# Local-attention layers on one core: the scores in tiles of 64 rows by 32 columns from one dense copy of the keys

## The reference, cut to what matters

```python
q, k, v = split(x @ Wqkv)                    # each [8, 16 heads, 512, 64]
q = rotary(l2norm(q) * qs); k = rotary(l2norm(k) * ksc)
# windows of 32 queries; each looks at its own 32 keys and the 32 before
bk2 = look(bk)                               # [.., 16 windows, 64 keys, 64]
sim = einsum('bhwie,bhwje->bhwij', bq, bk2) * 8.0
sim = where(mask, -max, sim)                 # only the last 33 keys up to the query
out = einsum('bhwij,bhwje->bhwie', softmax(sim), bv2)
x = out @ Wo + x
```

## Time and profile before

| | before |
|---|---|
| median of three runs | 4502.78 us |
| the profiled execution | 4502.94 us |
| its span (first to last instruction) | 4501.1 us |
| PE matmul busy | 4176.2 us (93%) |
| DVE busy | 4087.6 us (91%) |
| ACT busy | 2794.1 us (62%) |
| POOL busy | 2806.5 us (62%) |
| scores, L1233 | 12288 matmuls, 383.6 us |

### The profile page before, as it was taken

One profiled execution on the slowest core, in us unless ns is written; L12 is line 12 of the kernel. 1 busy time (PEld: TensorE's weight loads), 2 busy tenths in 40 slices (PEclk: granted clock), 3 DMA queues, 4 the chain that ended last, 5 costly groups with the idle time before them and its releaser, 6 DMA issues. The chain is left out here.

```text
span 4501.1 us, 98228 instructions
## 1 busy us (share of the span) xinstructions
PE 4176.2 (93%) x35048; PEld 2719.8 (60%) x35048; DVE 4087.6 (91%) x5503; ACT 2794.1 (62%) x4035; POOL 2806.5 (62%) x4595
## 2 busy tenths in 40 slices
PE   5999999999879999999999999999999999999997
PEld 3555555555456666666666666666666666666664
DVE  5888888888779999999999999999999999999995
ACT  4666666666545666666666666666666666666663
POOL 3555555555456666667666766666666666666663
PEclk9999999999989999999999999999999999999998
DMA  1000000000010000100011000100001000001000
GB/s 54 3 6 5 3 3 5 5 3 3 17 36 17 16 16 20 36 19 16 15 31 28 15 17 15 32 27 17 17 19 38 17 16 17 19 18 36 16 16 14
DMA packets 173500, 81.29 MB, mean 18 GB/s; under 512 B 109120, under 2 KB 168512, under 8 KB 172224
## 3 DMA queue, kind: packets, MB, share of 16 engines
q1 hardware_dynamic: 173248, 78.08, 6.4%
HBM read 48.56 MB, written 16.91 MB: 15 GB/s over the span
## 5 line engine op out<-in xcount | busy, mean ns | idle before, releaser
L581 POOL TENSOR_TENSOR pn<-es,rden 128x1024 f32<-128x1024 f32 x192 | 366.3, 1908 | 694.0 <-DVE rden L912 694.0
L675 ACT ACTIVATE y<-ps 128x1024 f32<-128x1024 f32 x384 | 372.2, 1021 | 507.4 <-PE ps L1119 507.4
L565 POOL TENSOR_TENSOR t<-t,ardn 128x1024 f32<-128x1024 f32 x256 | 484.6, 1893 | 301.4 <-DVE ardn L797 301.4
L666 ACT ACTIVATE t<-ps,anm,srn 128x512 f32<-128x512 f32 x512 | 392.5, 770 | 274.8 <-DVE anm L806 274.8
L585 POOL TENSOR_TENSOR t<-t 128x1024 f32<-128x1024 f32 x192 | 454.4, 2367 | 88.3 <-DVE t L864 88.3
L864 DVE TENSOR_TENSOR t<-ps,tabl 128x512 f32<-128x512 f32 x768 | 490.5, 680 | 0.0
L862 DVE TENSOR_TENSOR t<-ps,tabl 128x1024 f32<-128x1024 f32 x384 | 466.8, 1216 | 16.6 <-ACT sq L691 13.4
L587 POOL TENSOR_TENSOR t<-t 128x1024 f32<-128x1024 f32 x192 | 452.7, 2358 | 2.4 <-DVE t L864 2.4
L966 DVE TENSOR_TENSOR qn<-t,rn 128x2048 f32<-128x2048 f32 x192 | 438.1, 2282 | 5.1 <-POOL rn L394 5.1
L922 DVE TENSOR_REDUCE ss<-sq 128x32 f32<-128x2048 f32 x192 | 436.6, 2274 | 0.0
L996 PEld LDWEIGHTS ps<-cst,qn 128*128 128x128 f32 x3072 | 350.0, 141 | 114.2 <-issue 58.4
(11 more groups left out here) (138 smaller groups left out, 8859.4 us busy)
## 6 DMA issues: line engine op xcount, KB each, us to landing
tokens_dram<-x SPq DMA_DIRECT2D x96, 128.0 KB
xs<-tokens_dram SPq DMA_DIRECT2D x192, 64.0 KB, 1.8
xw<-tokens_dram SPq DMA_DIRECT2D x192, 64.0 KB, 1.9
xsh<-x SPq DMA_DIRECT2D x48, 128.0 KB
xsh<-x SPq DMA_DIRECT2D x48, 127.0 KB
wm<-in_l_wqk SPq DMA_DIRECT2D x3, 1024.0 KB, 4.9
wv<-in_l_wv SPq DMA_DIRECT2D x6, 512.0 KB, 3.8
wo<-in_l_wo SPq DMA_DIRECT2D x6, 512.0 KB, 4.6
```

Source lines behind the costliest of these rows:

```text
L565: nc.gpsimd.tensor_tensor(eA[:, v], eA[:, v], ardn[:, v].unsqueeze(2).to_broadcast([P, 2, SEQ]), ALU.mult).then_inc(a_pn, 1)
L666: e = act.activation(eA[:, j, h], bank(j % 2 * 2 + h), ACT.Exp, bias=anm[:, j, h:h + 1], scale=srn[:, a % 2, j, h:h + 1], accum_out=aden[: ...
```

## The change

The scores are computed with 64 rows, one head at a time. `kpad` becomes `kT`: 8 pairs x 544 columns, two heads one above the other in the rows as in `qT`, no zeros between. The buffer behind it (`kbuf`) keeps the size that the attention part needs. The two ACT copies of 64 partitions x 1024 become one of 128 x 1024, and the memset covers only the 32 columns before the first window of each pair. Each score matmul takes the 64 rows of one head, 32 queries as weights, and streams 64 key columns; there are 64 of them in a turn (128 instructions) in place of 32 (64 instructions). Even heads go to the first bank of pool1, odd heads to the second, so that scores and everything behind them stand in the order of `slot`, and the fold's result is read straight.

```diff
-        kpad = sb("kpad", [P, H, WIN + SEQ])
+        kbuf = sb("kbuf", [P, 4 * NU * SEQ])
+        kT = kbuf[:, 0:PAIRS * (WIN + SEQ)].rearrange("p (a c) -> p a c", a=PAIRS)
-            nc.gpsimd.memset(kpad[:], 0.0).then_inc(s_zero, 1)
+            nc.gpsimd.memset(kT[:, :, 0:WIN], 0.0).then_inc(s_zero, 1)
-                    act.activation(*keys(0, (c + 2) % NU), ACT.Copy)
-                    act.activation(*keys(1, (c + 2) % NU), ACT.Copy).then_inc(l_kT, 1)
+                    u = (c + 2) % NU
+                    act.activation(kT[:, :, WIN + u * P:WIN + (u + 1) * P], pool2.rearrange("p (a c) -> p a c", a=PAIRS),
+                                   ACT.Copy).then_inc(l_kT, 1)
-                            m = nc.tensor.matmul(ps_o, y[:, h], mhL[s.v][:, slot(h)], start=(h == 0), stop=(h == H - 1))
+                            m = nc.tensor.matmul(ps_o, y[:, h], mhL[s.v][:, h], start=(h == 0), stop=(h == H - 1))
                     for a in range(PAIRS):
-                        for w in range(NW):
-                            key0 = u * P + w * WIN
-                            m = nc.tensor.matmul(pool1[w * WIN:(w + 1) * WIN, a * 2 * KEYS:(a + 1) * 2 * KEYS],
-                                                 qT[:, a, w * WIN:(w + 1) * WIN], kpad[:, 2 * a:2 * a + 2, key0:key0 + KEYS],
-                                                 start=False, stop=True, skip_group_check=True)
+                        for odd in range(2):
+                            rows = slice(odd * DH, (odd + 1) * DH)
+                            for w in range(NW):
+                                key0 = u * P + w * WIN
+                                m = nc.tensor.matmul(pool1[w * WIN:(w + 1) * WIN, odd * 512 + a * KEYS:odd * 512 + (a + 1) * KEYS],
+                                                     qT[rows, a, w * WIN:(w + 1) * WIN], kT[rows, a, key0:key0 + KEYS],
+                                                     start=False, stop=True, skip_group_check=True)
```

More of the change, by code:

```diff
@@ L183, in build @@
         wqkA = wqkL[0].rearrange("p (a c) -> p a c", a=PAIRS)
+        kT = kbuf[:, 0:PAIRS * (WIN + SEQ)].rearrange("p (a c) -> p a c", a=PAIRS)
         eA = t12[:].rearrange("p (j s k) -> p j s k", j=NU, s=2)
-        pTA = kpad[:].rearrange("p h c -> p (h c)")[:, 0:4 * NU * SEQ].rearrange("p (v s k q) -> p v s k q", v=2, s=2, k=NU)
+        pTA = kbuf[:, 0:4 * NU * SEQ].rearrange("p (v s k q) -> p v s k q", v=2, s=2, k=NU)
         qkA = qn[:].rearrange("p (v u c) -> p v u c", v=2, u=NU)
@@ L321, in build @@
         s_out = sem("s_out")
[L323 to L327, removed]
         def layers(eng, turn):
```

## The result

| | before | after |
|---|---|---|
| median | 4503.59 us (4 runs, 4502.63 to 4506.17) | 4566.75 us (4 runs, 4562.36 to 4573.99) |
| ratio, 95% interval | | 1.0141 [1.0123, 1.0158] |
| profiled execution, span | 4502.94, 4501.1 us | 4573.99, 4572.2 us |
| mean granted clock | 0.991 | 0.978 |
| at 1.2 GHz between 1300 and 4400 us | 17.1 us, 4 stretches | 126.3 us, 33 stretches |

The kernel became 63 us slower where 20 us faster were forecast. The profiled execution of the kernel after is the slowest of its four, 7 us above their median; counts from its trace, such as the 33 stretches, hold for that execution. (In the kernel after, the scores are L1231, `windows_times` L1115, the transposes of q and k L992, the rotation L858 and L860, `mx` L952, `den` L906, `pT` L933.)

The account below looks back on a forecast made before the run. DVE was taken as the bound, a faster PE giving back about 60 us at most. Terms -28 (scores' waits), -4 (exponential), +12 (clock) make -20 us on 4502.94: 4483 us, own range 4467 to 4500, overall range 4462 to 4514.

Parts of the forecast that it names:

- the change by itself, on DVE: DVE's shorter waits: 28 us at the scores and 4 us at the exponential, a gain of 32 us.
- the clock's falls: PE's longer wait for pT when c = 0 lowers its clock: 10 falls at 1.2 us, 12 us lost.
- The scores: Scores on PE: 128 instructions on eight tiles take 1.15 us a turn instead of 1.95, PE gains 0.80 us.
- R1: Rival: eight tiles might not run beside each other, scores stay 1.95 to 2.0 us; 4503 us, chance 0.13.
- R3: Rival: each score instruction keeps its 0.0265 us, scores take 3.6 us; 4722 us, chance 0.08.
- a wait of 0.30 us: DVE's wait for the scores when c = 1: all 30 go, 9.0 us gained.
- those of 0.87: DVE's 14 waits for the scores in turns around the fold: each loses 0.80 us, 11.2 us gained.
- two fast bias turns: Two of six bias turns, at full clock: DVE's wait shrinks 0.8 us each, 1.6 us gained.
- four slow ones: Four bias turns at 1.2 GHz: scores take 2.1 us instead of 3.55, 5.8 us gained.
- 4 us forecast at the exponential: DVE's wait for the exponential ending turn c = 1: 0.1 us gained 43 times, 4 us.
- falls tend to drive themselves out: PE's clock when c = 0: a fall shifts the next stall to another moment; 10 falls chosen between 0 and 48.
- R2: Rival: clock falls in most turns c = 0, at `windows_times` and projections; 4529 us (4548 at 1.6 us each), chance 0.12.

Follow-up runs that it names:

- e4: Changed kernel with the loop over batches 2 to 6 written out and an extra unread matmul before `windows_times` when c = 0: 4468.56 us, ratio 0.9925.
- e9: Kernel before, without the change, with the loop over batches written out and the extra matmul before `windows_times` when c = 0: 4495.28 us, ratio 0.9982.
- e3: Changed kernel with one extra 128 x 512 matmul, result unread, before `windows_times` in turns with c = 0: 4511.1 us, ratio 1.0016.
- e1: Kernel before with each score matmul cut in two, same keys, columns, tiles and copies, 1760 PE instructions a pass: 4546.8 us, ratio 1.0094.
- e2: Changed kernel with the loop over batches 2 to 6 written out, nothing else different: 4491.1 us, ratio 0.9975.
- e6: Changed kernel with loop written out and extra matmul, keys copied again by two ACT instructions of 64 partitions: 4468.19 us, ratio 0.9926.

## Why the prediction was wrong

The runs divide the 63 us, by medians and rounded:

| term | forecast | measured | from |
|---|---|---|---|
| the change by itself, on DVE | -32 | -27 | e4 less e9 |
| the loop's stall | none | +43 | e3's +8.6 over before, with -27 taken off, is 35; 8 more for the stalls that e3 moved |
| the clock's falls | 10 at 1.2: +12 | 28 more at 1.7: +48 | after less e3 is 56, less the same 8 |
| sum | -20 | +64 | |

The three terms add up by the way they are made; the sum is no check. What bears them out stands apart from it: e1 loses 44 us without the change, the kernel after has 41.3 us of stalls behind the 24 jumps, and the batches of its trace give 1.7 to 2.1 us for a fall. The order matters too. Written out first, the loop gives 75.6 us (e2) and the matmul 22.5; the other way round it is 55.6 (e3) and 42.5. The division holds to some 10 us, not better.

**What bounds the kernel.** Right: DVE is the bound, and what it waits for tells where the time went. From before to after, over the whole of the layers (1262 to 4500 before, to 4570 after), its waits for the exponential, the square of k and the scores change by 54 + 47 - 7 = 94 us, and the 0.8 us that it had to spare at L924 are partly used up: that instruction's busy time falls by 19 us. Together they are 75 us, and the span grew by 71.

**The scores.** The term was mis-sized: 1.15 us forecast, 1.48 measured. The prediction had the pace from columns (16 rounds of 0.055 us) and the start of `windows_times` (4 ns an instruction over 0.03 us) as a bound of 1.2. The measured pace is (1.48 - 0.22) / 127 = 9.9 ns for a matmul and its weight load, 5 ns each: the bound was nearer than the value taken, and still 0.28 us short, since it was drawn from a burst of eight. e1 confirms the column pace where it is the limit (32 rounds of 0.055 and the tail, 1.98; measured 1.99). R1 is out: eight tiles do run beside each other. R3 is out as well. The floor of about 25 ns from start to start, which the Trainium skill gives in "TensorE: Matmul & The Clock Gate" (Part 1) and from which 3.4 us would follow, does not hold here across tiles: the trace has 9.9 ns.

**What DVE gets.** With 1.48 us, a wait of 0.30 us still goes, but those of 0.87 lose 0.47 instead of 0.80: 14 x 0.33 = 4.6 us less. The two fast bias turns give 0.7 less and the four slow ones, with 2.7 us instead of 2.1, 2.4 less. 32 - 7.7 = 24 us, against 27 in e4 and e9. The parts agree less well than the sum. DVE's waits for the scores are 42.6 us in e9 and 24.5 in e4, 18 less where this working has 20.5. The 4 us forecast at the exponential did not come: that wait goes from 12.6 to 17.6 us. The rest of the gain lies in smaller waits that the prediction did not name, so its agreement is in part luck.

**The keys' copy, the memset.** Costed at nothing. e6 shows it for the copy, with the loop written out and the matmul in; the memset was not tried.

**The clock.** The place was right: 24 of the 33 falls come with or right behind the wait of `windows_times` for pT. Of the others six are in the bias turns and three at the long stalls of the first layer. Number and price were not right. The stall is 2.00 us, not 2.5, in part since the scores are longer than thought, and this is enough. The step that failed is "falls tend to drive themselves out": the fall at 2064 us comes again at 2133 and 2201, and twice five batches in succession have one (from 2539 and from 3624 us). It is no rule either way: of 34 stalls of 1.9 to 2.3 us for pT, 21 had a fall. The rival R2 described this. It asked for 27 falls at this place and got 24, and 29 more than before in all, but had a chance of 0.12; its 4529 to 4548 us lack the loop's stall. A fall costs 1.7 us and more (22.5 / 12 = 1.9 between e2 and e4), not 1.2: from the slow `windows_times` the delay goes by y, exponential and `den`, whose wait grew from 15.4 to 66.4 us.

**The missing term.** This is the other step that failed, and the larger miss (43 us against 36 for the falls), since it was put at nothing: no step of the working, and no rival, asked what 128 instructions instead of 64 in each turn do to the program. The change "removes no instruction and adds none" is said of the order of heads alone; the doubling itself was priced only as the scores' pace. The loop's body went from 1248 to 1760 instructions of PE, and PE stands behind 20 of the 24 jumps back, for 41.3 us. e1 shows this without the change, e2 shows it gone without the loop. That the stall is the loading of instructions is argued, not shown: it is read from its place behind a jump, its cause "issue", the queue's packets, and the same stall in the kernel before at the jump of the much longer outer loop. Why the first layer's copy has the longest stalls and the last one's has none stays open.

The two debits also meet. Three of the four long stalls of the first layer have a fall with them, in the kernel after as in e1, and with the loop written out the falls go from 33 to 19. How the one feeds the other is not settled.

## What to carry to other kernels

Before an edit that doubles the instructions of a hot stage, count the instructions of each engine in the loop's body, before and after. The old trace gave one hint: a stall with the cause "issue" behind a jump back, here the 1.3 us of the outer loop. Where an engine that is not the bound becomes faster and waits longer, its clock may fall at the same place in pass after pass, and the engine that is the bound pays. An idle matmul in that wait gave back 56 us here, of which some 48 are falls, and nothing in the kernel that had few. An edit that small can also move the stalls of a loop from one copy of its code to another, so a comparison that rests on it has to look at them. The version with the change, the loop written out and that matmul takes 4468.6 us, 0.75% under the kernel before; with two copies of the keys it takes the same.

## What the runs showed of the hardware

- PE stood 1.2 to 4.8 us behind 20 of 24 jumps back of a loop with 1760 of its instructions, 2.2 to 3.2 us behind 8 of 24 with 1696, and at 1632 once, for 1.1 us. Layers that run the same copy of the code had the same stalls. Written out, a program with almost as many packets on the instruction queue (361 against 368) had no such stalls in these batches.
- Matmuls of 64 rows x 32 columns in eight tiles follow each other every 9.9 ns, weight load included; with half the columns streamed, the 128 of them take 1.29 us instead of 1.49.
- Of 34 stalls of PE of 1.9 to 2.3 us for pT, 21 had the granted clock fall to 1.2 GHz with or right behind them, up to five batches in succession; none of the 30 stalls of 1.66 to 1.71 us at the same place in the kernel before did. A fall cost the kernel 1.7 to 2.1 us, 0.9 to 1.0 in the last layer.
